# The scan's decay products as pairs in the rounded format, in a two-layer kernel on one core

## The chip, the cores and the metric

The kernel runs on one core of a Trainium2 chip. The metric is the device time of one execution in microseconds; the numbers given are medians of several runs. Engines are named as in the profile: PE is TensorE (matmul; PEld its weight loads), DVE is VectorE, ACT is ScalarE, POOL is GpSimd, SP is SyncE, which here only issues DMAs.

## The reference

Two layers on x of shape (2, 512, 256), each `x + s * silu(g)` of two branches. The first layer's branches are a Mamba-2 scan and a mixture of eight experts of which two are chosen per token; the second's are grouped-query attention and a sign-quantized linear layer. The part around the change is the scan, whose decays are exponentials of cumulative sums of logarithmic steps:

```python
dt = softplus(dt_raw + dt_bias)
log_a = -exp(A_log) * dt                       # per token and head (4 heads)
cum_log_a = cumsum(log_a, within a chunk)
L = exp(cum_log_a[i] - cum_log_a[j])           # j <= i, else 0
y_intra = L * (C @ B.T) * dt @ x
decay_to_end = exp(chunk_log_decay - cum_log_a)
state = decay * state + (decay_to_end * dt * B).T @ x
y_inter = exp(cum_log_a) * C @ state
y = (y_intra + y_inter + D * x) * silu(gate);  s = x_residual + y @ out_proj_w
```

## The kernel before, in words

Tokens are in eight tiles of 128, four for each of the two sequences. The stages in order of time are: layer norm, transposes and input projections (to about 65 us); a stage in which 23 expert tiles and the eight scan chunks (128 tokens each, `c` = 0 to 7) run side by side (to about 300 us); sums, second layer norm and attention (the rest).

Each engine has its own program, and the order inside the side-by-side stage is written out by hand. `side_by_side()` gives every step a due time in quarters of an expert tile and sorts; each engine walks the list and takes its own steps. For chunk `c` with `a = CHUNK_AT[c]` (3, 14.5, 26, ...) the steps of interest are:

```python
z += [(a - 4, "POOL", "D", c), (a + 0.5, "PE", "F", c), (a + 1, "ACT", "F", c), (a + 1.5, "PE", "C", c), ...
      (a + 2.5, "DVE", "C", c), (a + 3, "POOL", "C", c), (a + 5.5, "PE", "Y", c), (a + 6.5, "DVE", "Y", c), (a + 7.4, "ACT", "O", c),
      (a + 8.4, "DVE", "L", c)]
```

"D" on GpSimd is `decay(c)` (L1415): it multiplies the mask `upto` (128x128, ones where row <= column) with the chunk's logarithmic steps `dts[:, 7, c, :]`, broadcast over columns, into `decay_in`, 128x512 fp32 (four heads of 128). "F" on TensorE is `scan_decay(c)` (L1611, L1612): two fp32 matmuls of `decay_in`, with the weights `after` (into bank 4) and `ones` (into bank 5). "F" on ScalarE takes the exponentials of both banks, `within` and `since` (L1193, L1194). With them VectorE makes `x_dt` and `x_end`, GpSimd makes `mix` and, in chunks that carry a state, `c_dec` (L1434, L1436), and TensorE's "Y" (L1636 to L1641) makes the chunk's output and its state. VectorE's "Y" then scales and adds the state (L884, L887), forms dx (L891) and the gated output (L892); ScalarE makes its upper part `y_hi` (L1182), VectorE its lower part `y_lo` (L897), and TensorE's `out_rows` multiplies both with the output weights (L1530 to L1532, `split3`). `decay(c)` waits for the chunk before to have finished its decay matmuls, since it writes into the same buffer.

The expert steps around them are the matmuls on L1670 (hidden rows) and L1704 (back), the product of VectorE on L951, the gathers on L1425 and the scatters on L1459 of GpSimd. Weights of experts come by SP into three buffers (L509 and following). L845 is VectorE's convolution, L1402 GpSimd's first tap of it.

The rounded format is `float32r` (F32R): the kernel already writes many operands as an upper part, rounded to that format, and a lower part, the rest. The input projections (L1594, through L1530 to L1532) are such products, 128x512 each.

The logarithmic steps of all tiles are made once, in `finish_dt` on VectorE, at L747 to L757, while the projections run. `dts` has eight slots of 128x32; slot 6 is dt, slot 7 the logarithmic steps. `first` is a map of SBUF addresses that hold the tables of the router (`route` to `in_lane`) and are unused after the experts' tables are made.

Of the kernel before, what the change touches and what calls it, by code (L numbers as in the profile page):

```python
# [5 lines left out]
F32R = mybir.dt.float32r  # L6
# [5 lines left out]
P = 128  # L12
BATCH, SEQ, C = 2, 512, 256
T = BATCH * SEQ
NT = T // P
# [4 lines left out]
DI, NH = 512, 4  # L20
# [150 lines left out]
def layered_kernel(nc, x, params, consts, select, rope, w_in, w_out, w_moe, w_moe_tail, w_qkv, w_o, w_sign, out):  # L171
    ALU = mybir.AluOpType
# [3 lines left out]
    with ctx:  # L176
# [3 lines left out]
        def sb(name, shape, dt=F32, scope=ctx):  # L180
            return scope.enter_context(nc.sbuf_tensor(name, shape, dt))

        bank = [ctx.enter_context(nc.psum_tensor(f"bank{i}", [P, HALF], F32)) for i in range(8)]
# [3 lines left out]
        ident, upto, after = cst[:, 0:P], cst[:, P:2 * P], cst[:, 2 * P:3 * P]  # L187
        expert_no = cst[:, 3 * P:3 * P + E]
        ones = sb("ones", [P, P])
# [54 lines left out]
        CT = both("CT", [P, T])  # L244
        dtB = both("dtB", [P, NT, NH + P])
        dts = both("dts", [P, 8, NT, NH])
        a_neg = both("a_neg", [P, NH])


        weights_at = top_at - 3 * (FULL * WM + KC * P + C) * 4  # L250
        first = Map(both.at)
# [4 lines left out]
        hT_hi = first("hT_hi", [P, KC, T], F32R)  # L256
        hT_lo = first("hT_lo", [P, KC, T], F32R)
        ssm = first("ssm", [P, NCH, TAPS - 1 + SEQ])
        route = first("route", [P, NT, E])
        top = first("top", [P, NT, E])  # L260
        topi = first("topi", [P, NT, E], U32)
# [8 lines left out]
        picked = first("picked", [P, NT, 2, E])  # L270
        slot_f = first("slot_f", [P, NT * 2])
        in_lane = first("in_lane", [P, NT * 2])
        count_i = first("count_i", [P, NJ + 1 + P + 4 * NT + NJ], I32)
        count_f = first("count_f", [P, NJ + 1 + P + 4 * NT + NJ])
        weight_f = first("weight_f", [P, NT, 2])
# [3 lines left out]
        assert first.at <= weights_at  # L279
        w_out_sb = Map(top_at - NCH * C * 4)("w_out_sb", [P, NCH, C])  # L280
        picks = Map(hT_at + 2 * KC * T * 4)("picks", [P, PICKED, NT, P], F32R)
        zeros = gate[:, 0, 0:C]
        table = Map(both.at)
        lanes = table("lanes", [P, NT * 2, P])
# [13 lines left out]

        scan = Map(both.at)
        xg = scan("xg", [P, XR, C])  # L300
        decay_in = scan("decay_in", [P, NH, P])
        w_end = scan("w_end", [P, NH])
        dx = scan("dx", [P, NCH, P])
        state = scan("state", [P, NH, P])
# [93 lines left out]
        def sems(names):  # L398
            return (sem(n) for n in names.split())
# [7 lines left out]
        var_ready, root_ready, stat_ready, aggr_ready, xn_ready, h_ready, tr_full, hi_done, lo_done, ones_ready = sems(  # L407
            "var_ready root_ready stat_ready aggr_ready xn_ready h_ready tr_full hi_done lo_done ones_ready")
# [3 lines left out]
        dt_asked, dt_given, dt_ready, ssm_in, conv_start, conv_done, xs_ready = sems(  # L412
            "dt_asked dt_given dt_ready ssm_in conv_start conv_done xs_ready")

        decay_ready, decay_full, exps_ready, cb_full, cbm_ready, xt_full, xdt_ready, xend_ready, mix_ready, cdec_ready = sems(
            "decay_ready decay_full exps_ready cb_full cbm_ready xt_full xdt_ready xend_ready mix_ready cdec_ready")
# [38 lines left out]
        def stepper(eng, signal):  # L455

            n = [0]

            def then(ins):
                n[0] += 1  # L460
                ins.then_inc(signal, 1)
                eng.wait_ge(signal, n[0])
            return then

        vec = nc.vector
        TT, TS, STT = vec.tensor_tensor, vec.tensor_scalar, vec.scalar_tensor_tensor
        pool = nc.gpsimd
        mm = nc.tensor.matmul
# [189 lines left out]
        def _(dve):  # L658
            then = stepper(dve, vstep)
# [62 lines left out]
            for k in range(KC * BATCH):  # L722
                b, c = k // KC, k % KC
# [11 lines left out]
            v, az, z, u, d, lg = (dts[:, i, :, :] for i in range(6))  # L735
            dt, la = dts[:, 6, :, :], dts[:, 7, :, :]
# [7 lines left out]
            def finish_dt():  # L744
                dve.wait_ge(dt_given, 3)
                dve.wait_ge(dt_asked, 2)
                then(TS(az, d, 0.0, None, ALU.is_equal))  # L747
                then(TT(d, d, az, ALU.add))
                then(TT(lg, lg, az, ALU.add))
                then(TT(lg, lg, z, ALU.mult))  # L750
                then(vec.reciprocal(u, d))
                then(TT(lg, lg, u, ALU.mult))
                then(TS(v, v, 0.0, None, ALU.max))
                then(TT(dt, v, lg, ALU.add))
                dve.wait_ge(dt_given, 1)
                then(TS(a_neg[:, :], a_neg[:, :], -1.0, None, ALU.mult))
                TT(la, dt, a_neg[:, :].unsqueeze(1).to_broadcast([P, NT, NH]), ALU.mult).then_inc(dt_ready, 1)  # L757

            def choose_experts():
                dve.wait_ge(route_full, 1)  # L760
# [76 lines left out]
            def taps(b, m):  # L837

                n = b * NCH + m
                cs = slice(b * HALF, (b + 1) * HALF)  # L840
                dve.wait_ge(conv_start, n + 1)
                if n == 0:
                    dve.wait_ge(ones_ready, 2)
                for j in range(TAPS - 1):
                    ins = STT(out=xs[:, m, cs], in0=ssm[:, m, j:j + SEQ], scalar=col("conv_w", m * TAPS + j),  # L845
                              in1=xs[:, m, cs], op0=ALU.mult, op1=ALU.add)
                    ins.then_inc(conv_done, 1)
                    dve.wait_ge(conv_done, (TAPS - 1) * n + j + 1)
# [7 lines left out]
            taps(0, 2)  # L856
            taps(0, 3)
            finish_dt()
            dve.wait_ge(pr_full, len(PROJS))
            vec.memset(hE[0:TAIL, :, FULL * P:HC * P], 0.0).then_inc(pad_zero, 1)  # L860

# [231 lines left out]
            for i in range(2):  # L1093
                for h in range(2):
                    hs = slice(h * 32, (h + 1) * 32)
                    ins = TT(qT[(2 + i) * 32:(3 + i) * 32, 0, h, :], q_mix[hs, i, 0, :], q_hi[hs, i, :].bitcast(F32), ALU.subtract)
# [288 lines left out]
        def _(gp_):  # L1385
            GT = pool.tensor_tensor
# [21 lines left out]
            def decay(c):  # L1408

                if c > 0:  # L1410
                    gp_.wait_ge(decay_full, c)
                else:
                    gp_.wait_ge(dt_ready, 1)
                    gp_.wait_ge(pr_full, len(PROJS))
                GT(decay_in[:, :, :], upto.unsqueeze(1).to_broadcast([P, NH, P]),  # L1415
                   dts[:, 7, c, :].unsqueeze(2).to_broadcast([P, NH, P]), ALU.mult).then_inc(decay_ready, 1)

            def fetch(j):

# [104 lines left out]
        def _(pe):  # L1524
            def tr(dst, src):
                return nc.tensor.transpose(dst, src, ident)  # L1526

            def split3(dst, w_h, w_l, m_h, m_l, start, stop):

                mm(dst, w_l, m_h, start=start, stop=False)  # L1530
                mm(dst, w_h, m_l, start=False, stop=False)  # L1531
                return mm(dst, w_h, m_h, start=False, stop=stop)  # L1532
# [3 lines left out]
            for k in range(2 * KC * BATCH):  # L1536
                b, c = k // KC % BATCH, k % KC
                src, ready = (h_tok, h_ready) if k < KC * BATCH else (xn_tok, xn_ready)
                pe.wait_ge(ready, (b + 1) * TB)
                for t in range(TB):  # L1540
                    ins = tr(bank[k][:, t * P:(t + 1) * P], src[:, b * TB + t, c * P:(c + 1) * P])
# [5 lines left out]
            for t in range(NT):  # L1547
                if t > 1:
                    pe.wait_ge(dtb_taken, t - 1)
                for c in range(KC):  # L1550
                    ins = mm(bank[t % 2][:, 0:NH + P], hT[:, c, t * P:(t + 1) * P], w_in_sb[:, c, DT0:DT0 + NH + P],
                             start=c == 0, stop=c == KC - 1)
# [4 lines left out]
            for t in range(NT):  # L1557
                for c in range(KC):
                    ins = mm(bank[1][:, t * E:(t + 1) * E], xnT[:, c, t * P:(t + 1) * P],
                             par[:, PARAMS["gate_w"][0] + c * E:PARAMS["gate_w"][0] + (c + 1) * E], start=c == 0, stop=c == KC - 1)  # L1560
# [21 lines left out]
            for n, (b, kind, m) in enumerate(PROJS):  # L1582
# [10 lines left out]
                for c in range(KC):  # L1593
                    ins = split3(bk[:, :], w_in_hi[:, c, at:at + P], w_in_lo[:, c, at:at + P],  # L1594
                                 hT_hi[:, c, cs], hT_lo[:, c, cs], c == 0, c == KC - 1)
# [7 lines left out]

            def scan_decay(c):

                pe.wait_ge(decay_ready, c + 1)
                if c > 0:
                    pe.wait_ge(state_ready, c)
                    pe.wait_ge(s_part, c)
                dec = decay_in[:, :, :].rearrange("p h q -> p (h q)")  # L1610
                mm(bank[4][:, :], after, dec, start=True, stop=True)  # L1611
                mm(bank[5][:, :], ones[:, :], dec, start=True, stop=True).then_inc(decay_full, 1)  # L1612

            def scan_front(c):

# [132 lines left out]
            for i in range(3):  # L1748
                for t in range(TB):
                    ins = tr(bank[i][:, t * P:(t + 1) * P], rp4[:, i, t, :, :].rearrange("p h d -> p (h d)"))  # L1750
            ins.then_inc(turns_full, 1)
            pe.wait_ge(wsign_ready, KC)
            for k in range(KC):
                for m in range(KC):
                    ins = tr(bank[4][:, (k * KC + m) * P:(k * KC + m + 1) * P], wsg[:, m, k * P:(k + 1) * P])
# [156 lines left out]
            for n in range(NT // 2):  # L1912
                pe.wait_ge(sg_ready, KC * (n // (TB // 2) + 1))
                for j in range(2 * KC):
                    t, m = 2 * n + j // KC, j % KC
                    ins = tr(bank[n][:, j * P:(j + 1) * P], sT[:, m, t * P:(t + 1) * P])
# [74 lines left out]
```

## Time and profile before

| what | value |
| --- | --- |
| time, median of 3 runs (lowest, highest) | 755.84 us (753.89, 756.01) |
| the profiled execution | 756.22 us |
| its span from first to last instruction | 754.4 us |
| mean granted clock of TensorE | 0.984 of 2.4 GHz |
| TensorE busy | 711.2 us (94%), 4576 matmuls |
| VectorE, ScalarE, GpSimd busy | 65%, 55%, 51% of the span |
| decay matmuls (L1611, L1612) | 16 and 16 records |

A matmul's duration in the profile is modelled, from its start to the end of its results, and matmuls overlap; what one costs TensorE is the distance from its start to the next start. The chain of waits (the chain of work that ended last) does this already. A bracket at the end of a timeline row gives the time for which the engine stood idle before it and what released it. An fp32 matmul appears as two records.

### The profile page before, as it was taken

How to read it: one execution, taken by the hardware profiler on the slowest of the kernel's cores; microseconds unless marked ns; L12 is line 12 of the kernel's file. 1: busy time of each engine (PE TensorE's matmuls, PEld its weight loads, DVE VectorE, ACT ScalarE, POOL GpSimd, SP SyncE). 2: the span in 40 equal slices, each digit the busy share in tenths (PEclk: the TensorE clock that was granted, in tenths of full speed). 3: DMA queues.
4: the chain of work that ended last, by engine and by line, in shares of the span. 5: the costliest groups of instructions: out<-in, count | busy, mean ns of one | idle time of the engine just before them, and what ended most of it. 6: DMA issues, size and time to landing. Idle time of an engine off the chain costs nothing.

```text
span 754.4 us, 13451 instructions
## 1 busy us (share of the span) xinstructions
PE 711.2 (94%) x4576; PEld 622.9 (83%) x4576; DVE 489.7 (65%) x1036; ACT 416.7 (55%) x1043; POOL 384.5 (51%) x437
## 2 busy tenths in 40 slices
PE   2999999999999999699989999999999999999995
PEld 2887998988998888587778888888888888888884
DVE  7583555434323335898867777877777777777764
ACT  4436343242341342547667677767766677767662
POOL 1412442432323222137565777777876778677450
PEclk9899999999999999899999999999999999999998
DMA  8175877787878646145432332233222422132001
GB/s 293 41 227 179 284 247 236 230 254 250 252 239 246 196 140 170 33 115 183 115 106 53 89 81 53 65 77 82 65 57 72 92 67 63 46 85 57 2 1 56
DMA packets 103828, 98.06 MB, mean 130 GB/s; under 512 B 50576, under 2 KB 74064, under 8 KB 103632
## 3 DMA queue, kind: packets, MB, share of 16 engines
q1 hardware_dynamic: 101648, 91.43, 41.4%
q0 software_dynamic: 2112, 5.77, 2.3%
q8 instruction: 37, 0.61, 0.3%
q14 instruction: 31, 0.25, 0.1%
HBM read 69.24 MB, written 11.14 MB: 107 GB/s over the span
## 4 chain that ended last, share of the span: by engine, by line
PE 68%; DVE 11%; POOL 8%; ACT 8%; issue 4%; DMA 1%; SPq 0%; DVEq 0%; ACTq 0%; POOLq 0%
PE bank L1670 14%; PE bank L1530 8%; PE bank L1531 8%; PE bank L1532 8%; PE bank L1704 8%; PE bank L1526 8%; POOL prob L1488 4%; ACT prob L1294 3%; PE bank L1810 3%; PE bank L1811 3%; DVE nmax L1042 2%; ACT p_hi L1301 2%; POOL q_lo L1500 2%; DVE o_lo L1055 1%; PE bank L1813 1%
## 5 line engine op out<-in xcount | busy, mean ns | idle before, releaser
L1488 POOL TENSOR_TENSOR prob<-prob,rinv 128x128 f32<-128x128 f32 (+3 forms) x256 | 178.9, 731 | 106.4 <-DVE rinv L1047 106.4
L1294 ACT ACTIVATE prob<-bank,nmax 128x512 f32<-128x512 f32 (+3 forms) x256 | 133.4, 529 | 51.7 <-DVE nmax L1042 45.7
L1051 DVE TENSOR_TENSOR p_lo<-bank,p_hi 128x512 fp32r<-128x512 f32 x160 | 110.0, 687 | 48.8 <-ACT p_hi L1301 47.8
L1301 ACT ACTIVATE p_hi<-bank 128x512 fp32r<-128x512 f32 x160 | 96.3, 602 | 70.5 <-PE bank L1526 70.4
L1670 PEld LDWEIGHTS bank<-xgT,wm 128*128 128x128 f32 x920 | 108.7, 192 | 4.5 <-issue 2.9
L1670 PE MATMUL bank<-xgT,wm 128*128 128x128 f32 x920 | 111.3, 275 | 0.5 <-ACT xgT L1210 0.5
L1526 PE MATMUL bank<-cst,prob 128*128 128x128 f32 x640 | 97.4, 275 | 2.0 <-ACT prob L1294 1.2
L1042 DVE TENSOR_REDUCE nmax<-bank 128x1 f32<-128x512 f32 (+2 forms) x192 | 91.1, 502 | 6.2 <-PE bank L1813 5.5
L1530 PE MATMUL bank<-p_hi,v_lo 128*128 128x128 f32 (+3 forms) x256 | 92.8, 362 | 0.3 <-DVE p_lo L1051 0.3
L1810 PE MATMUL bank<-kT,qT 128*128 128x512 f32 (+3 forms) x256 | 81.5, 324 | 4.4 <-ACT prob L1294 4.3
L1459 POOL DMA_INDIRECT y_rows<-y_row,to_row x21 | 22.8, 1084 | 118.2 <-DVE y_row L911 92.5
L1532 PE MATMUL bank<-p_hi,v_hi 128*128 128x128 f32 (+3 forms) x256 | 82.2, 321 | 0.0
L1531 PE MATMUL bank<-p_lo,v_hi 128*128 128x128 f32 (+3 forms) x256 | 82.1, 321 | 0.0
L1526 PEld LDWEIGHTS bank<-cst,prob 128*128 128x128 f32 x640 | 73.3, 142 | 4.9 <-POOL prob L1488 2.1
L1811 PE MATMUL bank<-kT,qT 128*128 128x512 f32 (+3 forms) x256 | 74.4, 322 | 0.0
L1810 PEld LDWEIGHTS bank<-kT,qT 128*128 128x128 f32 x256 | 48.2, 188 | 13.3 <-issue 4.6
L1235 ACT ACTIVATE sil<-bank 128x512 f32<-128x512 f32 x23 | 13.7, 596 | 75.9 <-PE bank L1670 54.5
L1704 PE MATMUL bank<-wm,hE 128*128 128x256 f32 x230 | 53.5, 379 | 1.2 <-DVE y_low L916 1.2
L951 DVE TENSOR_TENSOR hE<-sil,bank 128x512 f32<-128x512 f32 x23 | 15.8, 687 | 57.5 <-PE bank L1670 40.6
L1294 ACT ACTIVATION_READ_ACCUMULATOR prob<-bank,nmax 128x1 f32 x256 | 52.3, 204 | 0.0
L1811 PEld LDWEIGHTS bank<-kT,qT 128*128 128x128 f32 x256 | 48.4, 189 | 4.1
L1532 PEld LDWEIGHTS bank<-p_hi,v_hi 128*128 128x128 f32 x256 | 48.3, 189 | 2.7
(309 smaller groups left out, 1529.3 us busy)
## 6 DMA issues: line engine op xcount, KB each, us to landing
wm<-in_w_moe SPq DMA_DIRECT2D x23, 1280.0 KB
wm<-in_w_moe SPq DMA_DIRECT2D x23, 640.0 KB
qT<-q_hi SPq DMA_DIRECT2D x124, 64.0 KB, 2.0
qT<-q_lo SPq DMA_DIRECT2D x124, 64.0 KB, 2.0
k_exp<-k_rows SPq DMA_DIRECT2D x56, 64.0 KB, 2.0
wtl<-in_w_moe_tail SPq DMA_DIRECT2D x46, 64.0 KB
y_rows<-gate SPq DMA_DIRECT2D x1, 2048.0 KB, 14.1
wq_raw<-in_w_qkv SPq DMA_DIRECT2D x32, 64.0 KB, 2.5
```

The costliest lines, as they stand in the source:

```text
L1051: TT(p_lo[:, b_, :], bank[2 + b_ % 2][:, :], p_hi[:, b_, :].bitcast(F32), ALU.subtract).then_inc(plo_done, 1)
L1294: ins = actv(prob[:, i % 2, h, POFF[j]:POFF[j] + (j + 1) * P], bk[:, at:at + (j + 1) * P], ACT.Exp, bias=nmax[:, i % 2, h, j:j + 1], accum ...
L1301: actv(p_hi[:, b_, :], bank[2 + b_ % 2][:, :], ACT.Copy).then_inc(phi_done, 1)
L1488: ins = GT(seg, seg, rinv[:, i % 2, k, j:j + 1].to_broadcast([P, (j + 1) * P]), ALU.mult)
L1526: return nc.tensor.transpose(dst, src, ident)
L1530: mm(dst, w_l, m_h, start=start, stop=False)
L1531: mm(dst, w_h, m_l, start=False, stop=False)
L1532: return mm(dst, w_h, m_h, start=False, stop=stop)
L1670: ins = mm(dst, w(c), xgT[:, u, c, :], start=c == 0, stop=c == KC - 1)
L1704: ins = mm(bank[3][:, 0:C], hE[:, u, i * P:(i + 1) * P], wm[:, s, i, PJ:WM] if i < FULL else ptl[:, s, :], start=i == 0, stop=i == HC - 1)
L1810: mm(dst, qs, kT[:, b, 0, 0:n], start=(h, j, at) == SCORES[k][0], stop=False)
L1811: mm(dst, qs, kT[:, b, 1, 0:n], start=False, stop=False)
```

## The change

The logarithmic steps `la` are split once into an upper part in the rounded format and a lower part, put into slots 0 and 3 of `dts`. GpSimd makes two products a chunk instead of one, `decay_hi` where `decay_in` was, and `decay_lo` where the router's tables were. The weights `after` and `ones` are copied into the rounded format once. TensorE makes each of its two decay products from two matmuls that add up in one bank, lower part first.

```diff
+        la_hi, la_lo = dts[:, 0, :, :].bitcast(F32R), dts[:, 3, :, :]
+        route_at = first.at
         route = first("route", [P, NT, E])
...
+        spent = first.at
         count_i = first("count_i", [P, NJ + 1 + P + 4 * NT + NJ], I32)
...
+        behind = Map(route_at)
+        decay_lo = behind("decay_lo", [P, NH, P], F32R)
+        after_r = behind("after_r", [P, P], F32R)
+        ones_r = behind("ones_r", [P, P], F32R)
...
-        decay_in = scan("decay_in", [P, NH, P])
+        decay_hi = scan("decay_hi", [P, NH, P], F32R)
...
-                TT(la, dt, a_neg[:, :].unsqueeze(1).to_broadcast([P, NT, NH]), ALU.mult).then_inc(dt_ready, 1)
+                then(TT(la, dt, a_neg[:, :].unsqueeze(1).to_broadcast([P, NT, NH]), ALU.mult))
+                then(vec.tensor_copy(la_hi, la))
+                TT(la_lo, la, dts[:, 0, :, :], ALU.subtract).then_inc(dt_ready, 1)
...
             finish_dt()
+            for to, what in ((after_r, after), (ones_r, ones[:, :])):
+                vec.tensor_copy(to[:, :], what).then_inc(ones_ready, 1)
             dve.wait_ge(pr_full, len(PROJS))
...
-                GT(decay_in[:, :, :], upto.unsqueeze(1).to_broadcast([P, NH, P]),
-                   dts[:, 7, c, :].unsqueeze(2).to_broadcast([P, NH, P]), ALU.mult).then_inc(decay_ready, 1)
+                for part, la in ((decay_hi, dts[:, 0, c, :]), (decay_lo, la_lo[:, c, :])):
+                    ins = GT(part[:, :, :], upto.unsqueeze(1).to_broadcast([P, NH, P]),
+                             la.unsqueeze(2).to_broadcast([P, NH, P]), ALU.mult)
+                ins.then_inc(decay_ready, 1)
...
+                if c == 0:
+                    pe.wait_ge(ones_ready, 5)
                 pe.wait_ge(decay_ready, c + 1)
...
-                dec = decay_in[:, :, :].rearrange("p h q -> p (h q)")
-                mm(bank[4][:, :], after, dec, start=True, stop=True)
-                mm(bank[5][:, :], ones[:, :], dec, start=True, stop=True).then_inc(decay_full, 1)
+                dec = [d[:, :, :].rearrange("p h q -> p (h q)") for d in (decay_lo, decay_hi)]
+                for dst, w in ((bank[4], after_r), (bank[5], ones_r)):
+                    for i in range(2):
+                        ins = mm(dst[:, :], w[:, :], dec[i], start=i == 0, stop=i == 1)
+                ins.then_inc(decay_full, 1)
```

## Rows read from the trace of the kernel before

**Rows 1.** The page: busy time of the engines, and the granted clock in 40 slices.

```profile
PE 711.2 (94%) x4576; PEld 622.9 (83%) x4576; DVE 489.7 (65%) x1036; ACT 416.7 (55%) x1043; POOL 384.5 (51%) x437
...
PEclk9899999999999999899999999999999999999998
```

**Rows 2.** Busy times by stretch: start:end, length, engines' busy us, clock, DMA share, GB/s.

```profile
66.00:300.00 234.00, 230.77 (x1646) 209.98 (x1647) 98.53 (x200) 82.38 (x178) 73.86 (x67) 1.00 0.73 227
```

**Rows 3.** Waits of the SP queue, 65 to 312 us: total us, times, longest.

```profile
SPq L509 <- PE bank L1670: 81.9, 20, 6.4
```

**Rows 4.** Instructions that write or read decay_in: duration ns min/median/max, first and last start.

```profile
L1611 PE MATMUL bank<-decay_in,cst x16: 592/594/667, 71.6 to 274.8; 128*128 128x512 f32 x16
...
L1415 POOL TENSOR_TENSOR decay_in<-cst,dts x8: 1040/1050/1053, 64.9 to 266.4; 128x512 f32<-128x512 f32 x8
```

**Rows 5.** Chain that ended last, chunk 0: start, us, what.

```profile
71.76 0.86 PE bank L1611 x2
72.62 0.86 PE bank L1612 x2
```

**Rows 6.** Timeline of the projections: start us, us, engine, line, operation.

```profile
61.80 0.39 PE L1530 MATMUL bank<-hT_hi,w_in_lo 128*128 128x512 f32 x1
...
62.50 0.39 PE L1530 MATMUL bank<-hT_hi,w_in_lo 128*128 128x512 f32 x1
```

**Rows 7.** Timeline, lower parts of y in chunks 3 and 4.

```profile
176.99 1.05 POOL L1415 TENSOR_TENSOR decay_in<-cst,dts 128x512 f32<-128x512 f32 x1
...
178.16 0.68 DVE L897 TENSOR_TENSOR y_lo<-gate,y_hi 128x512 fp32r<-128x512 f32 x1
...
178.90 0.39 PE L1530 MATMUL bank<-w_out_hi,y_lo 128*128 128x256 f32 x1
...
206.05 1.05 POOL L1415 TENSOR_TENSOR decay_in<-cst,dts 128x512 f32<-128x512 f32 x1
...
207.23 0.68 DVE L897 TENSOR_TENSOR y_lo<-gate,y_hi 128x512 fp32r<-128x512 f32 x1
...
207.97 0.39 PE L1530 MATMUL bank<-w_out_hi,y_lo 128*128 128x256 f32 x1
...
208.20 0.28 PE L1531 MATMUL bank<-w_out_lo,y_hi 128*128 128x256 f32 x1
...
208.32 0.28 PE L1532 MATMUL bank<-w_out_hi,y_hi 128*128 128x256 f32 x1
```

**Rows 8.** Timeline, before the first expert tile and chunk 0.

```profile
64.86 0.27 DVE L860 MEMSET hE<- 64x256 f32 x1 [2.83 <-PE bank L1532]
64.90 1.04 POOL L1415 TENSOR_TENSOR decay_in<-cst,dts 128x512 f32<-128x512 f32 x1 [5.22 <-PE bank L1532]
...
71.60 0.59 PE L1611 MATMUL bank<-decay_in,cst 128*128 128x512 f32 x1
```

**Rows 9.** Timeline, GpSimd and VectorE in chunks 1 and 2; a later GpSimd subtraction.

```profile
114.49 1.05 POOL L1415 TENSOR_TENSOR decay_in<-cst,dts 128x512 f32<-128x512 f32 x1
114.53 1.57 DVE L884 TENSOR_TENSOR state<-state,since 128x512 f32<-128x512 f32 x1 [0.92 <-DVE xs L845]
...
143.84 1.05 POOL L1415 TENSOR_TENSOR decay_in<-cst,dts 128x512 f32<-128x512 f32 x1
144.53 0.91 DVE L892 TENSOR_TENSOR gate<-dx,gate 128x512 f32<-128x512 f32 x1
...
300.16 1.28 POOL L1454 TENSOR_TENSOR wk_lo<-wk,wk_hi 128x512 fp32r<-128x512 f32 x1 [1.80 <-DVE xs L965]
```

**Rows 10.** The line that scales the state: duration ns min/median/max.

```profile
L884 DVE TENSOR_TENSOR state<-state,since x6: 680/692/1571, 114.5 to 288.2; 128x512 f32<-128x512 f32 x6
```

**Rows 11.** Timeline, chunk 3: ScalarE's exponentials, and TensorE behind GpSimd.

```profile
157.99 1.28 ACT L1193 ACT_TABLE_LOAD   x1
...
159.28 0.60 ACT L1193 ACTIVATE within<-bank 128x512 f32<-128x512 f32 x1
...
168.20 0.35 PE L1636 MATMUL bank<-mix,x_dt 128*128 128x128 f32 x1 [0.73 <-POOL c_dec L1436]
```

More of the change, by code:

```diff
@@ L281, in layered_kernel @@
         picks = Map(hT_at + 2 * KC * T * 4)("picks", [P, PICKED, NT, P], F32R)
+        behind = Map(route_at)
+        decay_lo = behind("decay_lo", [P, NH, P], F32R)
+        after_r = behind("after_r", [P, P], F32R)
+        ones_r = behind("ones_r", [P, P], F32R)
+        assert behind.at <= spent
         zeros = gate[:, 0, 0:C]
```

## The prediction

> **What bounds the kernel now.** I read the page first, for the share of each engine and the granted clock; then busy times by stretch for the stage that holds the change; then the two edited matmul lines and the edited product; then the timeline around each of the eight chunks. On the page TensorE is busy 94% of the span, and its busy tenths are at nine in nearly every slice [rows 1]. From 66 to 300 us, where experts and scan run side by side, it is busy 230.77 of 234.00 us at a granted clock of 1.00 (the 2.4 GHz level); VectorE has 98.5, ScalarE 82.4 and GpSimd 73.9 us there [rows 2]. So the order written out for TensorE sets this stage, and only 3.2 us of it is waiting. The weights don't set it: the SP queue spends 81.9 us waiting for TensorE to free the buffer of hidden weights, 20 times [rows 3]. All that comes later starts from what this stage leaves, so time taken off TensorE here should come off the end.
>
> **What it removes.** Each fp32 product is issued as two passes: 16 records on L1611 (and as many on L1612) are eight chunks times two, with a median of 594 ns by their modelled ends [rows 4]. The modelled ends overlap, so I use the distance between starts. The chain gives 0.86 us to each pair on L1611 and on L1612, that is 0.43 us a pass [rows 5]. A chunk's four passes take 1.72 us, and eight chunks 13.8 us. Nothing covers them: neighbouring matmuls stand directly before and behind.
>
> **What it adds on TensorE.** Also four matmuls, now in the rounded format, 128x512 each, two products with each of two weights. The projections run this shape in the same format: from 61.80 to 62.50 us four of them start, three gaps in 0.70 us, so 0.233 us apart, each with other weights than the one before [rows 6]. Four take 0.93 us, eight chunks 7.5 us. The number of instructions stays. The difference is 13.8 - 7.5 = 6.3 us. For entering the rounded format behind fp32 matmuls I take nothing; as a bound, the first of the output product's matmuls at 207.97 us starts 0.23 us before its successor where the next stands 0.12 apart [rows 7], 0.1 us a chunk or 0.9 us in all. I take none because that row also stands behind a wait.
>
> **Setting up.** VectorE gets four more instructions around the logarithmic steps: a copy and a subtraction of 128x32 and two copies of 128x128. The nearest row, the memset on L860, takes 0.27 us, so about 1.1 us with all four. VectorE is idle for 2.83 us before L860 because the projections are unfinished, and the first decay product on GpSimd waits 5.22 us for the same thing [rows 8]. Cost nothing; without that cover 1.1 us, once. The new wait of TensorE on five marks is met long before 71.60 us. The two-product step before chunk 0 ends near 67.0 us, still 4.6 us before TensorE asks [rows 8].
>
> **What it adds on GpSimd.** A second product per chunk, 1.05 us like the first [rows 4], at most 1.28 us, which a 128x512 GpSimd operation writing the rounded format takes with two full inputs [rows 9]. That is 8.4 us (10.2 at most) on an engine a third busy. The products for chunks 1 to 7 start a tile or more before they are used, and what is queued behind (gathers three tiles ahead, first taps) has as much room. In itself that costs nothing.
>
> **What it disturbs.** VectorE's scaling of the state takes 680 ns at least and 692 in the median, but 1571 ns once [rows 10], at 114.53 us, where it starts 0.04 us behind the decay product; it ends 0.56 us after that product does. The gate product at 144.53 us takes 0.91 instead of 0.69 us, again ending behind a decay product [rows 9]. Both read two inputs from SBUF. So such an instruction on VectorE is held while GpSimd multiplies. Now the second product lengthens each such window to 2.1 us. At 178.16 us VectorE starts the lower part of y (gate and y_hi, both in SBUF), which TensorE waits for; the decay product of chunk 4 ended at 178.04. In the changed kernel the second one runs 178.02 to 179.07, so the lower part is held 0.9 us, and with it L1530, which started at 178.90 directly behind it. Chunk 5 is the same: product 206.05 to 207.10, lower part 207.23, TensorE 207.97; held until 208.13, 0.9 us [rows 7]. At the other six I find no VectorE instruction with two SBUF inputs in the added microsecond on which TensorE stands at once: at 114.53 the scaling could be held up to 1.05 us more, but the next reader is two tiles away. So 2 x 0.9 = 1.8 us is given back, between 0 (VectorE slips in first) and 2.1 (each a whole 1.05 us).
> This is also what the Trainium skill says (SBUF — State Buffer, "Who interferes with whom"): a VectorE instruction with two SBUF inputs contends with a GpSimd one that reads SBUF, and whoever came first holds the port for its whole length, the other being blocked. By that rule, the trace agrees (1571 against 692 ns), and the sum below stands; without it the sum would be the full 6.3 us.
>
> **Sum.** -6.3 + 1.8 + 0 (set-up, entry, gathers) = -4.5 us. The profiled execution took 756.22 us (span 754.4 and 1.8 around it), so 751.7; from the median 755.84, 751.3 us. The likeliest case's own range takes entry at 0 to 0.9 us and the hold at 1.2 to 2.1: a gain of 3.3 to 5.1, 750.7 to 752.5 us.
>
> **Rivals.**
> Full gain. The y_lo hold doesn't fall on TensorE's path, since ordering or arrival shifts by a microsecond as TensorE runs earlier. For: the clearance at 178 and 207 us is just 0.12 us, and the added window is one microsecond wide. Against: both sides are started by the same TensorE events, so they move together. Gain 6.3: 749.5 us. Chance 0.22.
> The gain is absorbed: a chain that doesn't begin at the decay matmuls becomes the limit. In chunk 3 ScalarE's table load starts at 157.99 us, right after its last silu, and the exponential at 159.28 follows the load, not the matmul; TensorE later waits 0.73 us for c_dec on GpSimd [rows 11]. If TensorE comes 0.79 us earlier and such a chain does not, that chunk loses its share. For: that wait. Against: this GpSimd chain starts from a result of TensorE after the decay products (y_row), so it moves too, and other chunks show no such wait. If five of eight shares go (3.9 of 6.3) with the 1.8, the gain is 0.6: 755.2 us. Chance 0.18.
> No faster matmuls: the rounded products run at the 0.43 us of fp32. Then nothing is gained and the hold costs 1.8: 757.6 us. Against are the projections [rows 6]. Chance 0.02.
> Slower by collision: the second decay product holds a VectorE instruction on TensorE's path in every chunk. Place: GpSimd's L1415 step; price 1.05 to 1.28 us a chunk, 8.4 to 10.2 us, less 6.3: 2.1 to 3.9 slower, 757.9 to 759.7. It decides from six chunks of eight (6.3 / 1.05). I find two. Chance 0.04.
>
> **How the numbers follow.** Forecast 0.54, the rivals as above. Within about 0.3% (2.3 us) a measurement of this kernel can't tell a difference. Faster by over 0.3% holds the forecast, the full gain and a little of the absorbed case: 0.78. Same: most of the absorbed case and half of the next: 0.17. Slower: 0.05. The range reaches from the full gain less 0.7 us of spread (the three runs lie 2.1 us apart) to the absorbed case: 748.8 to 755.2 us. Predicted: 751.4 us.
>
> **What would show it.** Four records per chunk on the decay matmul line, 0.23 us apart. Two records of 1.05 us per chunk on the GpSimd line. The stage of 66 to 300 us shorter by 4 to 5 us with TensorE as busy as now. Lower parts of y in chunks 3 and 4 of about 1.6 us instead of 0.68 where they start within a second product, with an idle TensorE behind. If these two stay at 0.68, the full gain. The prediction is wrong if idle time of TensorE in the stage grows by more than 2 us, if the rounded matmuls stand 0.43 us apart, or if the attention stage behind 315 us changes its length.

## The result, and the profile after

Six runs of the changed kernel have a median of 750.37 us (749.87 to 751.91), the kernel before, in six, 754.16 us (753.89 to 756.01). The ratio is 0.9943 with a 95% interval of 0.993 to 0.9957: faster by 0.57%, or 4.3 us of some 754 (3.2 to 5.3); the two medians themselves are 3.8 us apart. Forecast were 751.4 us and a gain of 4.5. The profiled execution took 750.26 us with a span of 748.4; the lines of the kernel have moved by 8 to 18 (L1611 and L1612 are L1629 now, L1415 is L1428, L1530 is L1544, L884 is L896, L892 is L904, L897 is L909).

The page, as [rows 1]:

```profile
PE 704.3 (94%) x4575; PEld 622.4 (83%) x4576; DVE 493.9 (66%) x1040; ACT 416.3 (56%) x1043; POOL 392.0 (52%) x445
...
PEclk9999999999999999899999999999999999999998
```

TensorE is 6.9 us less busy (1.1 us of it before the stage with the change, where the clock differs, see below), VectorE 4.2 and GpSimd 7.5 us more. The matmuls and products by tile, `decay_hi` and then `decay_lo`, as [rows 4]:

```profile
L1428 POOL TENSOR_TENSOR decay_hi<-cst,dts x8: 1039/1047/1052, 63.3 to 260.8; 128x512 fp32r<-128x512 f32 x8
...
L1629 PE MATMUL bank<-decay_hi,after_r x8: 392/394/399, 70.2 to 269.0; 128*128 128x512 f32 x8
```

```profile
L1428 POOL TENSOR_TENSOR decay_lo<-cst,dts x8: 1039/1042/1047, 64.3 to 261.8; 128x512 fp32r<-128x512 f32 x8
```

The chain of work at chunk 0, as [rows 5], and the timeline of TensorE there:

```profile
70.15 0.93 PE bank L1629 x4
```

```profile
69.91 0.48 PE L1629 MATMUL bank<-decay_lo,after_r 128*128 128x512 f32 x1
70.22 0.40 PE L1629 MATMUL bank<-decay_hi,after_r 128*128 128x512 f32 x1
70.45 0.39 PE L1629 MATMUL bank<-decay_lo,ones_r 128*128 128x512 f32 x1
70.68 0.39 PE L1629 MATMUL bank<-decay_hi,ones_r 128*128 128x512 f32 x1
70.91 1.28 PE L1688 MATMUL bank<-xgT,wm 128*128 128x128 f32 x10
```

Four rounded matmuls take 0.93 us of the chain where two fp32 products took twice 0.86. The starts are 0.23 us apart behind the first. By the starts in the trace, the first rounded one follows the matmul before it by 0.03 us, where the first fp32 pass followed by 0.11 us. From the matmul before the decay products to the one behind them it is 1.83 us before and 1.04 to 1.07 us now (in chunk 1, where it takes some 0.26 us longer in both, 2.10 and 1.31). Over eight chunks that is 6.26 us less.

The lower parts of y in chunks 3 and 4, as [rows 7]; the bracket is the engine's idle time and what ended it:

```profile
172.21 1.05 POOL L1428 TENSOR_TENSOR decay_hi<-cst,dts 128x512 fp32r<-128x512 f32 x1
...
173.20 1.05 POOL L1428 TENSOR_TENSOR decay_lo<-cst,dts 128x512 fp32r<-128x512 f32 x1
...
173.38 1.42 DVE L909 TENSOR_TENSOR y_lo<-gate,y_hi 128x512 fp32r<-128x512 f32 x1
...
174.87 0.38 PE L1544 MATMUL bank<-w_out_hi,y_lo 128*128 128x256 f32 x1 [0.84 <-DVE y_lo L909]
...
202.26 1.04 POOL L1428 TENSOR_TENSOR decay_lo<-cst,dts 128x512 fp32r<-128x512 f32 x1
...
202.44 1.43 DVE L909 TENSOR_TENSOR y_lo<-gate,y_hi 128x512 fp32r<-128x512 f32 x1
...
203.91 0.38 PE L1544 MATMUL bank<-w_out_hi,y_lo 128*128 128x256 f32 x1 [0.84 <-DVE y_lo L909]
```

Both start within the second product, take 1.42 and 1.43 us instead of 0.68, and end 0.56 us behind it. TensorE stands idle for 0.84 us each time; some 0.10 us of that was there before (in the kernel before its last matmul ends at 178.80 us and L1530 starts at 178.90), so each hold costs it some 0.74 us. Chunks 1 and 2 on VectorE, as [rows 9]:

```profile
111.29 1.05 POOL L1428 TENSOR_TENSOR decay_hi<-cst,dts 128x512 fp32r<-128x512 f32 x1
111.33 2.56 DVE L896 TENSOR_TENSOR state<-state,since 128x512 f32<-128x512 f32 x1 [0.92 <-PE bank L1656]
...
139.84 0.68 DVE L903 TENSOR_TENSOR dx<-bank,dx 128x512 f32<-128x512 f32 x1
139.85 1.05 POOL L1428 TENSOR_TENSOR decay_hi<-cst,dts 128x512 fp32r<-128x512 f32 x1
140.55 1.90 DVE L904 TENSOR_TENSOR gate<-dx,gate 128x512 f32<-128x512 f32 x1
```

The state's scaling is held through both products, 2.56 us against 1.57 before, and the gate product 1.90 against 0.91. The dx instruction (L903) has one of its inputs in a bank of the matmul results and not in SBUF; it runs beside the first product and takes the usual 0.68 us. Nothing on TensorE waits for them: the waits of TensorE from 60 to 300 us name only one new reason, the first of these (columns: total us, times, longest):

```profile
PE bank L1544 <- DVE y_lo L909: 1.7, 2, 0.8
...
PE bank L1722 <- DVE y_low L928: 1.2, 1, 1.2
PE bank L1654 <- POOL c_dec L1450: 0.7, 1, 0.7
```

The set-up, as [rows 8]: VectorE's idle time before the memset has gone from 2.83 to 2.12 us, and GpSimd still waits 5.22 us for the projections.

```profile
63.25 0.27 DVE L872 MEMSET hE<- 64x256 f32 x1 [2.12 <-PE bank L1546]
63.29 1.04 POOL L1428 TENSOR_TENSOR decay_hi<-cst,dts 128x512 fp32r<-128x512 f32 x1 [5.22 <-PE bank L1546]
```

**The length of the stage.** The spans of the two profiles differ by 6.0 us, more than the medians. The first decay product starts at 63.29 us here and at 64.90 before, so 1.6 us of that lie ahead of the stage with the change; the last experiment shows that the kernel before can start at either time. I therefore measure the stage from the start of that product to the start of GpSimd's `wv_lo`, the first subtraction for the weights of the second layer. These are the second marks, of the kernel before and of the changed one:

```profile
295.98 2.38 POOL L1451 TENSOR_TENSOR wv_lo<-wv,wv_hi 128x1024 fp32r<-128x1024 f32 x1 [11.34 <-DVE xs L965]
```

```profile
289.61 2.38 POOL L1465 TENSOR_TENSOR wv_lo<-wv,wv_hi 128x1024 fp32r<-128x1024 f32 x1 [11.34 <-DVE xs L977]
```

Before, 295.98 - 64.90 = 231.08 us; changed, 289.61 - 63.29 = 226.32 us: 4.76 us less. Busy times between the two marks, as [rows 2], of the kernel before and of the changed one:

```profile
64.90:295.98 231.08, 227.16 (x1623) 206.74 (x1624) 96.25 (x196) 82.94 (x179) 72.52 (x68) 1.00 0.74 230
```

```profile
63.29:289.61 226.32, 220.93 (x1623) 206.72 (x1624) 99.58 (x196) 82.99 (x179) 80.31 (x76) 1.00 0.76 234
```

TensorE is busy for 6.23 us less and idle for 1.47 us more (3.92 and 5.39 us): the two sides of the change. From the second mark to the end of the span it is 458.4 and 458.8 us; over the ten profiles of this study it is 458.1 to 459.0, with and without the edit, so the rest has kept its length.

### The profile page after: what moved, and what is told of

Its sections match the earlier page's. It is cut to its first block, busy times and chain, and to the rows that moved or that the text cites. A ratio compares the mean times of both kernels' runs of the same rounds, so it can differ in the third digit from the quotient of the medians.

```text
span 748.4 us, 13463 instructions
## 1 busy us (share of the span) xinstructions
PE 704.3 (94%) x4575; PEld 622.4 (83%) x4576; DVE 493.9 (66%) x1040; ACT 416.3 (56%) x1043; POOL 392.0 (52%) x445
## 4 chain that ended last, share of the span: by engine, by line
PE 68%; DVE 11%; POOL 8%; ACT 7%; issue 4%; DMA 1%; SPq 0%; ACTq 0%; DVEq 0%
PE bank L1688 14%; PE bank L1540 8%; PE bank L1544 8%; PE bank L1545 8%; PE bank L1546 8%; PE bank L1722 8%; POOL prob L1502 4%; ACT prob L1306 3%; PE bank L1828 3%; PE bank L1829 3%; DVE nmax L1054 2%; ACT p_hi L1313 2%; POOL q_lo L1514 2%; DVE o_lo L1067 1%; PE bank L1831 1%
## 5 line engine op out<-in xcount | busy, mean ns | idle before, releaser
L1544 PE MATMUL bank<-p_hi,v_lo 128*128 128x128 f32 (+3 forms) x256 | 92.9, 363 | 0.3 <-DVE p_lo L1063 0.3
```

## The experiments

Ratios are against the runs of the kernel before that were taken on the same chip beside them (medians of 754.16 us for the changed kernel, 755.63 for the four below it, 755.84 for the last ones). The stage is that between the two marks, in the one profiled execution of each kernel. The profile of "changed" is the one above. The first four experiments ran on one chip and the others on another, and their stages are compared across the two.

| kernel | median us | ratio (95%) | stage us | against before |
| --- | --- | --- | --- | --- |
| before | 754.16 | 1 | 231.08 | |
| changed | 750.37 | 0.9943 (0.993 to 0.9957) | 226.32 | -4.76 |
| lo_after_y | 748.67 | 0.9918 (0.9903 to 0.9934) | 224.87 | -6.21 |
| one_product | 750.72 | 0.9937 (0.9923 to 0.995) | 224.82 | -6.26 |
| old_matmuls | 756.41 | 1.002 (1.001 to 1.0031) | 232.52 | +1.44 |
| fill | 749.43 | 0.9922 (0.9906 to 0.9938) | 224.62 | -6.46 |
| three_products | 750.15 | 0.9932 (0.9915 to 0.9948) | 226.32 | -4.76 |
| three_matmuls | 747.12 | 0.9894 (0.9872 to 0.9915) | 222.89 | -8.19 |
| before_look1 | one run, 754.88 | | 231.19 | |
| before_look2 | one run, 755.87 | | 231.05 | |

The stage repeats within 0.14 us for the kernel before (three profiles), so it tells differences that the medians, which move by 2 us between runs, leave open.

### lo_after_y: the lower product behind the lower part of y

```diff
                 for part, la in ((decay_hi, dts[:, 0, c, :]), (decay_lo, la_lo[:, c, :])):
+                    if part is decay_lo and c in (4, 5):
+                        gp_.wait_ge(y_lo_done, c)
                     ins = GT(part[:, :, :], ...
```

> The changed kernel, but in chunks 4 and 5 GpSimd's second (lower) product waits until VectorE has made the lower part of y of the chunk before. If the second product's hold on that VectorE instruction is what TensorE pays for, both lower parts take 0.68 us again, the two idle times of 0.84 us of TensorE go, and the kernel is 1.7 us below the changed one, at about 0.992 of the kernel before. If TensorE's wait there has another cause, or the microseconds come back as another wait, it stays at the changed kernel's 0.994 to 0.995.

Measured: 748.67 us, ratio 0.9918, the stage 1.45 us shorter than the changed kernel's. Its timeline at chunk 3:

```profile
172.12 1.05 POOL L1430 TENSOR_TENSOR decay_hi<-cst,dts 128x512 fp32r<-128x512 f32 x1
...
173.29 0.69 DVE L909 TENSOR_TENSOR y_lo<-gate,y_hi 128x512 fp32r<-128x512 f32 x1
...
174.03 0.38 PE L1546 MATMUL bank<-w_out_hi,y_lo 128*128 128x256 f32 x1
...
174.06 1.04 POOL L1430 TENSOR_TENSOR decay_lo<-cst,dts 128x512 fp32r<-128x512 f32 x1 [0.89 <-DVE y_lo L909]
```

The lower part takes 0.69 us, TensorE's two waits for it are gone from the list of waits, and nothing has come in their place. The product now waits itself, 0.89 us, on an engine that has the time. Between the marks TensorE is busy for 220.96 us and idle for 3.91, as long idle as in the kernel before:

```profile
63.20:288.07 224.87, 220.96 (x1623) 206.73 (x1624) 98.28 (x196) 83.00 (x179) 80.40 (x76) 1.00 0.76 236
```

The hold was the cause of the loss, and this is the fastest kernel of the study with the whole computation. The expectation had 1.7 us for it; it counted the whole idle time of 0.84 us at each place, of which 0.10 stands there without any hold.

### one_product: no second product

```diff
-                for part, la in ((decay_hi, dts[:, 0, c, :]), (decay_lo, la_lo[:, c, :])):
-                    ins = GT(part[:, :, :], ...
-                ins.then_inc(decay_ready, 1)
+                GT(decay_hi[:, :, :], ..., ALU.mult).then_inc(decay_ready, 1)
...
-                dec = [... for d in (decay_lo, decay_hi)]
+                dec = [... for d in (decay_hi, decay_hi)]
```

> The changed kernel with GpSimd's second product left out: the four rounded matmuls of a chunk all read the upper product (the decays are then those of twice the steps). If the gain is 6.3 us of TensorE less 1.7 of the hold, this one shows the whole 6.3: 0.9917 of the kernel before, the same as with the lower product delayed. If the additional GpSimd work costs in other places as well, it is clearly faster than the delayed one. If the rounded matmuls gain less than their start distances say, it stays near 0.994.

Measured: the stage is 224.82 us, like that of lo_after_y (224.87) to 0.05 us. So the second product costs nothing but the two holds: the other six are free. The ratio is a miss: 0.9937 is what the expectation gave to rounded matmuls that gain less, and 0.9917 was expected. The profiles say where this comes from. The profiled execution took 750.06 us, 2.04 more than that of lo_after_y: its stage starts 1.74 us later (at 64.94 us against 63.20, see the last experiment), and what follows the stage is 0.31 us longer. By medians alone this run would have been read wrongly.

### old_matmuls: the costs without the gain

```diff
-        decay_hi = scan("decay_hi", [P, NH, P], F32R)
+        decay_hi = scan("decay_hi", [P, NH, P])
...
-                for part, la in ((decay_hi, dts[:, 0, c, :]), (decay_lo, la_lo[:, c, :])):
+                for part, la in ((decay_hi, dts[:, 7, c, :]), (decay_lo, la_lo[:, c, :])):
...
+                dec = decay_hi[:, :, :].rearrange("p h q -> p (h q)")
+                mm(bank[4][:, :], after, dec, start=True, stop=True)
+                mm(bank[5][:, :], ones[:, :], dec, start=True, stop=True).then_inc(decay_full, 1)
```

> The changed kernel with the fp32 matmuls of before (which read a product of the unsplit steps); all else is kept: the split of the steps, the copies, the second product on GpSimd (nothing reads it). By the theory the costs stand here without the gain: the hold in chunks 3 and 4 gives 1.7 us more than before, 1.002. If the second product is free, 1.000. If part of the gain has nothing to do with the matmuls (an earlier start of the stage, say), it is below 1.000 by that part.

Measured: ratio 1.002 (1.001 to 1.0031), the stage 1.44 us longer than before. The lower parts of y are at 1.43 us in chunks 3 and 4 here as well, and TensorE's list of waits has the same line:

```profile
PE bank L1544 <- DVE y_lo L909: 1.7, 2, 0.8
```

So the ratio and the stage agree with the first branch of the expectation, if at 1.44 us for 1.7. The two halves of the change add up: +1.44 for the second product and, from one_product, -6.26 for the matmuls make -4.82; the changed kernel has -4.76.

### fill: GpSimd as busy, but reading nothing

```diff
-                for part, la in ((decay_hi, dts[:, 0, c, :]), (decay_lo, la_lo[:, c, :])):
-                    ins = GT(part[:, :, :], ...
-                ins.then_inc(decay_ready, 1)
+                GT(decay_hi[:, :, :], ..., ALU.mult)
+                pool.memset(decay_lo[:, :, :].bitcast(F32), 0.0).then_inc(pool_ready, 1)
+                gp_.wait_ge(pool_ready, 6 + c)
+                pool.memset(decay_lo[:, :, :].bitcast(F32), 0.0).then_inc(decay_ready, 1)
```

> The changed kernel with GpSimd's second product replaced by two fills with zero of the same 128x512 buffer, some 1 us together (the lower part of the decays is left out). They occupy GpSimd for as long as the product, but read nothing. If it is GpSimd's reading from SBUF that holds VectorE, the lower parts of y take 0.68 us and the time is that of the kernel without the second product, 0.9917. If any GpSimd instruction of that length holds it, they take about 1.4 us and the time is the changed kernel's 0.994 to 0.995.

Measured: the stage is 224.62 us, 0.2 us below those of the two kernels without the hold; that small rest is unexplained. Its timeline at chunk 3:

```profile
174.91 0.55 POOL L1429 MEMSET decay_lo<- 128x512 f32 x1
...
175.12 0.68 DVE L909 TENSOR_TENSOR y_lo<-gate,y_hi 128x512 fp32r<-128x512 f32 x1
...
175.51 0.52 POOL L1431 MEMSET decay_lo<- 128x512 f32 x1
```

The lower part of y starts within the first fill, runs beside it and into the second, and takes 0.68 us. Held by the first fill alone, and ending 0.56 us behind it as behind a product, it would have taken 0.90. The state's scaling in chunk 1, too, waits for the product only and not for the fills behind it: 1.57 us, as before. So it isn't GpSimd's being busy that holds VectorE; a GpSimd instruction that only writes SBUF doesn't hold it, and one that reads there does. (A fill differs from a product in its operation as well; that this matters was not tried apart.) The Trainium skill's rule (SBUF — State Buffer, "Who interferes with whom") makes just this difference, and the run agrees: 0.68 us beside fills, 1.42 beside a product.

### three_products: a gap between products

```diff
-                ins.then_inc(decay_ready, 1)
+                ins.then_inc(pool_ready, 1)
+                gp_.wait_ge(pool_ready, 6 + c)
+                GT(decay_lo[:, :, :], ..., ALU.mult).then_inc(decay_ready, 1)
```

> The changed kernel with the lower product made twice in a row on GpSimd, the second time behind a wait on its own semaphore. If GpSimd keeps VectorE out for as long as it reads, across products, the lower parts of y in chunks 3 and 4 take about 2.5 us and TensorE loses 1.0 us more at each: the side-by-side stage is 2.0 us longer than the changed kernel's. If VectorE is let in at the gap between two products, they stay at 1.4 us and the stage is as long as the changed kernel's. The other six chunks add nothing in either case; a stage longer by 4 us and more would show that they are near the path.

Measured: the stage is 226.32 us, exactly the changed kernel's. Its timeline at chunk 3:

```profile
173.24 1.05 POOL L1428 TENSOR_TENSOR decay_lo<-cst,dts 128x512 fp32r<-128x512 f32 x1
...
173.41 1.43 DVE L909 TENSOR_TENSOR y_lo<-gate,y_hi 128x512 fp32r<-128x512 f32 x1
...
174.36 1.38 POOL L1432 TENSOR_TENSOR decay_lo<-cst,dts 128x512 fp32r<-128x512 f32 x1
```

Now it is GpSimd that is held: its third product takes 1.38 us, since VectorE was let in at the gap that the semaphore wait leaves. In the same run, at chunk 1, both cases stand side by side:

```profile
111.31 1.05 POOL L1428 TENSOR_TENSOR decay_hi<-cst,dts 128x512 fp32r<-128x512 f32 x1
111.35 2.56 DVE L896 TENSOR_TENSOR state<-state,since 128x512 f32<-128x512 f32 x1 [0.92 <-DVE xs L855]
112.31 1.04 POOL L1428 TENSOR_TENSOR decay_lo<-cst,dts 128x512 fp32r<-128x512 f32 x1
113.43 1.38 POOL L1432 TENSOR_TENSOR decay_lo<-cst,dts 128x512 fp32r<-128x512 f32 x1
```

The first two products follow each other without a wait, 1.00 us from start to start, and the state's scaling is held through both, though it began 0.96 us ahead of the second; ahead of the third it is let in. So who came first doesn't decide it alone, as the prediction's words on the rule would have it: the gap does too. A third product of 1 us in each chunk costs the stage nothing, so GpSimd has room at all eight places; what counts is which VectorE instruction stands beside it.

### three_matmuls: is TensorE's order still the limit?

```diff
-                    for i in range(2):
-                        ins = mm(dst[:, :], w[:, :], dec[i], start=i == 0, stop=i == 1)
+                    for i in range(2) if w is after_r else (1,):
+                        ins = mm(dst[:, :], w[:, :], dec[i], start=i == 0 or w is ones_r, stop=i == 1)
```

This is lo_after_y with one matmul fewer in each chunk.

> The kernel with the delayed lower product, and with the lower matmul of the second decay product left out (three rounded matmuls a chunk; its decays are those of the upper part). If TensorE's order still bounds the stage, it is shorter by 8 times 0.23, 1.9 us, than with the delay alone: 223.0 us from the first decay product to the first subtraction for the weights of the second layer, ratio about 0.989. If another engine's chain has become the limit, it is shorter by less than 1 us.

Measured: 222.89 us, 1.98 us below lo_after_y, where eight times 0.233 is 1.86. Time taken off TensorE still comes off the stage one for one; the second of this kernel's two decay products lacks its lower part, so it is a measure and no candidate.

### The kernel before, run twice more

> The kernel before, unchanged. The side-by-side stage takes 231.1 us again. If the start of the stage (64.9 us in the profile of before, 63.3 in that of the changed kernel) depends on when TensorE's granted clock comes back in the projections and not on the edit, this one may start at either; if it is the edit, it starts at 64.9.

> The same once more, since the runs of before lie in two clusters, at 754.2 and 755.9 us: a start of the stage at 63.3 us with 754.2, or at 64.9 us with 755.9.

Measured: stages of 231.19 and 231.05 us, starting at 63.52 and 64.99 us, with 754.88 and 755.87 us. So the start varies without any edit. Busy times from 28 to 34 us, within the projections (the column before the last two is the granted clock), first of before_look1, then of before_look2:

```profile
28.00:34.00 6.00, 6.00 (x22) 4.78 (x22) 3.29 (x32) 2.70 (x5) 0.95 (x2) 0.72 0.00 0
```

```profile
28.00:34.00 6.00, 6.00 (x17) 4.94 (x18) 3.30 (x32) 2.21 (x4) 0.25 (x1) 0.50 0.00 0
```

In the second, the clock is at its lower level (1.2 GHz) in the whole stretch, and 17 matmuls are issued; in the first it is there for a part, and 22 are. The profile of before has 0.50 in this stretch, that of the changed kernel 0.72. All ten profiles fall into these two groups: at 0.72 the stage starts at 63.20 to 63.52 us (changed, lo_after_y, old_matmuls, three_products, three_matmuls, before_look1), at 0.50 at 64.90 to 65.03 (before, one_product, fill, before_look2). Both groups hold kernels with and without the edit, so I count the 1.6 us as this and not as part of the change.

## Why the prediction was right

**The stage is bound by TensorE.** Shown: the stage loses what its matmuls lose, in three kernels of different length (-6.26 without the second product, -6.21 with it delayed, and 1.98 more with a matmul fewer in each chunk).

**-6.3 us for the matmuls.** Measured -6.26 in one_product and -6.21 in lo_after_y. Distances between starts were the right measure: from the matmul before the decay products to the one behind them they give 6.24 us in both kernels. Modelled durations would have given 5.7 us: 32 records of 0.593 us less 8 of 0.478 and 24 of 0.393.

**Entering the rounded format: nothing.** The second of the four starts 0.31 us behind the first, not 0.23, which alone would be the 0.1 us that the prediction had as a bound. But the first starts only 0.03 us behind the matmul before it, 0.08 us sooner than an fp32 pass did, which makes up for it; the chain counts 0.93 for all four, and the stage bears that out.

**+1.8 us for the hold.** Measured +1.44 (old_matmuls), 1.45 (the difference that the delay makes) and 1.50 (the difference to one_product). The mechanism and the two places were right: chunks 3 and 4, and only these. The size was 0.3 to 0.4 us too large in all, since I let the held instruction run its whole 0.68 us after the product's end; it ends 0.56 us behind it, and the second product starts 1.00, not 1.03 us, behind the first. The state's scaling in [rows 9] showed the first of these already.

**Set-up, gathers, the remaining six chunks: nothing.** For gathers and chunks shown by one_product and three_products. For the set-up the starts of the stage show it: at the same granted clock the kernels with it start at 63.20 to 63.50 us and before_look1, without it, at 63.52.

**The sum.** -6.3 + 1.8 = -4.5 was forecast; -4.76 us is the stage's, 4.3 (3.2 to 5.3) that of the runs. The absolute 751.4 us was too high by 1.0 us: it stood on a median of three runs, 755.84, where six give 754.16; from that the same sum gives 749.7, too low by 0.7. That the absolute time came within 1.0 us is in part luck: its base moved by 1.7 us between three runs and six, more than any term of the sum was off. The 0.26 us between the sum and the stage are the hold's, which was smaller than forecast.

**The rivals.** The full gain falls by the 1.42 us of y_lo, and is what lo_after_y gets. The absorbed gain falls: TensorE's wait for c_dec is 0.7 us before and after, no longer. Matmuls at the pace of fp32 fall by the starts 0.23 us apart. A hold in every chunk falls by the list of waits: VectorE was held at four places, TensorE waited at two.

## What to carry to other kernels

When GpSimd gets another instruction that reads SBUF, list what VectorE does in the added window, mark those with two inputs from SBUF, and ask of each who waits for it; only that costs, not GpSimd's load. Here a VectorE instruction with one input in a bank (L903) and one beside a GpSimd fill were not held. Where a held one is on the path, put the GpSimd instruction behind it with a wait on the semaphore that it signals anyway: two lines gave 1.45 us here. And compare a stage between two marks inside it when medians move by more than the effect.

## What the runs showed of the hardware

- Two GpSimd products without a wait between them held the state's scaling on VectorE through both (2.56 us), though it began before the second; where a semaphore wait stood between two, VectorE was let in and GpSimd's next product took 1.38 instead of 1.05 us.
- A held VectorE instruction ends 0.56 us after the product, not 0.68, its whole length: so at all four places in the changed kernel, whether it began 0.04 or 0.7 us behind the start of a product. Why is not shown.
- In seven of eight chunks the first rounded matmul starts 0.03 us behind the matmul before it, and the second 0.31 to 0.32 us behind the first; the rest stand some 0.23 us apart. The first fp32 pass started 0.11 us behind the matmul before it, and the passes stood 0.43 us apart.
- The kernel before starts its second stage at 63.5 or 65.0 us, as TensorE's granted clock is at 0.72 or 0.50 from 28 to 34 us; in both cases TensorE had been busy for 13 to 14 of the 28 us ahead of that. The times of its profiled executions, 754.88 us with the early start and 755.87 and 756.22 with the late one, fit this, but three of them don't show that its two clusters of times, at 754.2 and 755.9 us, come from it. What decides the clock from run to run was not tried.
